# Second attention: output products in three passes behind the next pair's first scores, and all full key tiles split

## What is computed

```python
def rmsnorm(x, g): return x * rsqrt(mean(x*x) + 1e-5) * g
q = (layernorm(x) @ Wq).reshape(b, Sq, 16, 128)     # 256 queries a batch
k = (ctx @ Wk).reshape(b, Skv, 16, 128)             # 1601 keys a batch
v = (ctx @ Wv).reshape(b, Skv, 16, 128)
scores = einsum('bqhd,bkhd->bhqk', rmsnorm(q, gq), rmsnorm(k, gk)) * 128**-0.5
out = einsum('bhqk,bkhd->bqhd', softmax(scores), v)
x = x + tanh(g) * (out.reshape(b, Sq, 2048) @ Wo)
```

## Time and profile before

| | |
|---|---|
| median of 3 runs | 1923.51 us (1918.31 to 1924.34) |
| profiled execution: its own time, its span | 1915.69 us, 1914.0 us |
| TensorE / VectorE / ScalarE / GpSimd busy | 95% / 71% / 61% / 18% of the span |
| granted clock of TensorE, mean | 0.984 |

### The profile page before, as it was taken

How to read it: one execution, slowest core, us unless ns; L and a number is a source line. 1 busy time by engine, 2 the same in 40 slices (tenths; PEclk the granted TensorE clock), 3 DMA queues, 4 the chain that set the end, 5 groups by cost and what they waited for, 6 DMA issues and landing times.

```text
span 1914.0 us, 31506 instructions
## 1 busy us (share of the span) xinstructions
PE 1808.8 (95%) x9091; PEld 1327.3 (69%) x9091; DVE 1368.0 (71%) x2282; ACT 1165.7 (61%) x1946; POOL 340.1 (18%) x301
## 2 busy tenths in 40 slices
PE   5789898989999999999999999999999998999998
PEld 3344444558888677776777767777677776788887
DVE  8565656455665787887878878788688886666665
ACT  2576776843333677777877768777687774232232
POOL 3010101214443300001000010000100003444452
PEclk9899999989999999999999999999999998999999
DMA  3414232345443200001000010000000001455543
GB/s 97 108 30 96 54 72 51 75 160 132 112 112 79 69 1 0 0 0 35 1 0 0 0 35 1 0 0 0 1 1 0 0 0 47 102 115 115 113 111 77
DMA packets 108704, 95.80 MB, mean 50 GB/s; under 512 B 71796, under 2 KB 93176, under 8 KB 107992
## 3 DMA queue, kind: packets, MB, share of 16 engines
q1 hardware_dynamic: 108632, 94.88, 20.1%
HBM read 72.94 MB, written 1.44 MB: 39 GB/s over the span
## 4 chain that ended last, share of the span: by engine, by line
PE 80%; DVE 11%; ACT 2%; issue 2%; POOL 2%; SPq 1%; DMA 0%; ACTq 0%; DVEq 0%
PE ps L1213 28%; PE ps L451 17%; PE ps L462 8%; PE ps L1075 5%; PE ps L1287 4%; PE ps L1062 4%; PE ps L1308 3%; DVE s_rk L1847 3%; PE ps L1229 3%; PE ps L1000 2%; POOL s_p L786 2%; SPq L553 1%; PE ps L1303 1%; DVE s_rq L1843 1%; PE ps L1237 1%
## 5 line engine op out<-in xcount | busy, mean ns | idle before, releaser
L957 ACT ACTIVATE s_p<-ps,s_g,s_rk 128x256 f32<-128x256 f32 (+1 forms) x832 | 412.5, 560 | 120.3 <-PE ps L1213 91.1
L1213 PE MATMUL ps<-s_qq,s_ctxT 128*128 (+2 forms) x1248 | 385.4, 421 | 6.5 <-DVE s_qq L1836 5.0
L451 PE MATMUL ps<-s_xT,s_wgus 128*128 128x512 f32 x1440 | 349.9, 392 | 0.8 <-DVE s_hw L1740 0.8
L451 PEld LDWEIGHTS ps<-s_xT,s_wgus 128*128 128x128 f32 x1440 | 271.7, 189 | 60.1 <-DVE s_hw L1740 1.7
L1213 PEld LDWEIGHTS ps<-s_qq,s_ctxT 128*128 128x128 f32 (+1 forms) x1248 | 228.5, 184 | 93.0 <-issue 39.0
L1213 PE MATMUL ps<-s_ps,s_ctx 128*128 128x512 f32 x960 | 273.4, 394 | 0.1
L853 ACT ACTIVATE s_p<-ps,s_bsm 128x1024 f32<-128x1024 f32 x208 | 219.4, 1111 | 87.1 <-PE ps L1075 84.7
L1898 DVE TENSOR_TENSOR s_dsum<-s_dsum,s_p 128x512 f32<-128x512 f32 (+1 forms) x352 | 242.2, 688 | 26.8 <-ACT s_p L957 14.9
L1907 DVE TENSOR_TENSOR s_ps<-s_p,s_ps 128x512 fp32r<-128x512 f32 x320 | 220.0, 687 | 6.4 <-ACT s_ps L963 3.0
L1213 PEld LDWEIGHTS ps<-s_ps,s_ctx 128*128 128x128 f32 x960 | 180.0, 188 | 45.9 <-DVE s_ps L1907 1.8
L370 ACT CAST s_hs<-s_hw 128x512 fp32r<-128x512 f32 x120 | 74.5, 620 | 202.6 <-DVE s_hw L1740 202.6
(11 more groups left out here) (265 smaller groups left out, 2117.8 us busy)
## 6 DMA issues: line engine op xcount, KB each, us to landing
s_wB<-w1s SPq DMA_DIRECT2D x64, 256.0 KB, 3.9
s_kT<-s_kst SPq DMA_DIRECT2D x96, 128.0 KB, 2.3
s_kT<-s_kst SPq DMA_DIRECT2D x96, 80.0 KB, 2.1
s_wB<-w0s SPq DMA_DIRECT2D x15, 384.0 KB, 3.7
s_wB<-w0s SPq DMA_DIRECT2D x16, 256.0 KB, 3.9
s_wgu<-in_L_ffn_Wg_dram SPq DMA_DIRECT2D x64, 64.0 KB, 2.9
s_wgu<-in_L_ffn_Wu_dram SPq DMA_DIRECT2D x64, 64.0 KB, 2.6
s_wd<-in_L_ffn_Wd_dram SPq DMA_DIRECT2D x64, 64.0 KB, 2.6
```

The source lines that it names most:

```text
L451: ins = nc.tensor.matmul(ps[:, 4 + g, :], wgus[:, slot, w, g, k, :], xT[:, x_, k, n], start=c == 0, stop=c == len(ops) - 1)
L957: ins = nc.scalar.activation(p1[0:r, SLOT1[t], j, :], ps[0:r, BANK1[t], j * SQ:(j + 1) * SQ], ACT.Exp, bias=g1[0:r, 3:4], scale=rk_col(t, ...
L1213: ins = nc.tensor.matmul(out, lhs(x_), rhs(y_), start=first and n == 0, stop=last and n == 2)
```

## The change

1. **Tiles 3 and 7 are split too.** SPLIT1 is now tiles 0 to 11, only tile 12 stays plain. HI_DVE is tiles 1 and 6 (was 2, 6, 10), so ScalarE makes the high part of ten tiles (was seven). The ring ps1 has 4 slots (was 5).
2. **Output products in three passes.** oT1 becomes a high and a low part. ScalarE copies the high part from bank 4 (`take_sums`), VectorE subtracts for the low part (`low_sums`); it replaces VectorE's copy. M is kept in high and low parts, and the four plain matmuls become twelve float32r ones (line 1213's helper).
3. **They move.** TensorE's output products stand behind scores1(t = 3) of the next pair, ahead of scores1(4) and values1(0). ScalarE's copy stands behind the exponentials of tile 0 of the next pair and ahead of tile 0's high part. VectorE's subtraction stands first in the next pair. The first pair of a batch has none, and the last pair's stand behind the loop.
4. **M's parts ahead of the loop.** ScalarE copies eight high parts and four float32 copies (m1w); GpSimd subtracts for the first half (one instruction, 128 by 2048), VectorE for the second (four instructions of 512 columns, behind the layer norm). The layer norm's transposes use PSUM banks 4 to 7 instead of 0 to 3 and no longer wait for ScalarE's copies of M. One copy of ctx for each batch becomes smaller.

```diff
-SPLIT1 = (0, 1, 2, 4, 5, 6, 8, 9, 10, 11)
-HI_DVE = (2, 6, 10)
+SPLIT1 = tuple(range(KT - 1))
+HI_DVE = (1, 6)
-WHOLE1 = (3, 7, 12)
-RING1 = 5
+WHOLE1 = (12,)
+RING1 = 4
...
# GpSimd, ahead of the loop
+            pool.wait_ge(s.m1_read, 4)
+            n = slice(0, H1 * D // 2)
+            g_.tensor_tensor(m1[:, 1, n], m1w[:], m1[:, 0, n].bitcast(F32), ALU.subtract).then_inc(s.m1_rest, 1)
...
# ScalarE
+                def take_sums(hp):
+                    act.wait_ge(s.pv1, primed(at(KT * 8 * b, hp, KT, 0)))
+                    nc.scalar.copy(oT1[:, 0, :], ps[:, 4, :]).then_inc(s.o1_hi, 1)
...
                         ins.then_inc(s.probs1, 1)
+                        if t == 0 and not first:
+                            take_sums(hp)
                         if t in HI_ACT:
...
# TensorE
-            pe.wait_ge(s.m1_read, 8)
             pe_turn(pe, 2)
...
+                def outputs(hp):
+                    pe.wait_ge(s.o1_read, primed(hp + 8 * b))
+                    pe.wait_ge(s.y1_added, primed(hp + (8 * b - 1)))
+                    for j in range(4):
+                        ins = product(ps[:, 5 + j // 2, (j % 2) * D:(j % 2 + 1) * D], lambda part: oT1[:, part, j * P:(j + 1) * P],
+                                      lambda part: m1[:, part, bass.ds(hp * (2 * D) + (j // 2 - 2) * D, D)])
+                    ins.then_inc(s.y1_made, 1)
...
                         if t:
                             values1(hp, t - 1)
+                        elif not first:
+                            outputs(hp)
                     values1(hp, KT - 1)
...
-                    pe.wait_ge(s.o1_read, primed(hp + (8 * b + 1)))
-                    pe.wait_ge(s.y1_added, primed(hp + 8 * b))
-                    for j in range(4):
-                        ins = nc.tensor.matmul(ps[:, 5 + j // 2, (j % 2) * D:(j % 2 + 1) * D], oT1[:, j * P:(j + 1) * P],
-                                               m1[:].rearrange("p h n -> p (h n)")[:, bass.ds(hp * (2 * D) + (j // 2) * D, D)],
-                                               start=True, stop=True)
-                    ins.then_inc(s.y1_made, 1)
...
# VectorE
+            for j in range(4, 8):
+                n = slice(2 * D * j, 2 * D * (j + 1))
+                dve.wait_ge(s.m1_hi, j + 1)
+                v.tensor_tensor(m1[:, 1, n], ps[:, j % 4, :], m1[:, 0, n].bitcast(F32), ALU.subtract).then_inc(s.m1_low, 1)
...
+                def low_sums(hp):
+                    dve.wait_ge(s.o1_hi, at(8 * b, hp, 1, 0))
+                    v.tensor_tensor(oT1[:, 1, :], ps[:, 4, :], oT1[:, 0, :].bitcast(F32), ALU.subtract).then_inc(s.o1_read, 1)
...
                 def weights(hp, first):
+                    if not first:
+                        low_sums(hp)
                     for t in range(KT):
...
-                    dve.wait_ge(s.pv1, primed(at(k0, hp, KT, KT)))
-                    v.tensor_copy(oT1[:], ps[:, 4, :]).then_inc(s.o1_read, 1)
...
+                low_sums(H1 // 2)
                 finish(H1 // 2)
```

More of the change, by code:

```diff
@@ L270, in program @@
         p1 = sb("p1", [P, 5, 2, SQ], scope=se)
-        dsum = sb("dsum", [P, 2 * SQ], scope=se)
-        oT1 = sb("oT1", [P, 2 * SQ], scope=se)
-        m1 = sb("m1", [P, H1, D], scope=se)
+        m1 = sb("m1", [P, 2, H1 * D], F32R, scope=se)
         ctxT1 = sb("ctxT1", [P, 2, KV + 1], F32R, scope=se)
@@ L283, in program @@
         ps1 = sb("ps1", [P, RING1, 2, HALF], F32R, scope=se)
-        sb("ps1_rest", [P, H1 * P + KSQ * HALF - RING1 * 2 * HALF], scope=se)
+        dsum = sb("dsum", [P, 2 * SQ], scope=se)
+        oT1 = sb("oT1", [P, 2, 2 * SQ], F32R, scope=se)
         rd1 = sb("rd1", [P, 4], scope=se)
@@ L326, in program, with turn_bank @@
         of = out.rearrange("b s d -> (b s) d").rearrange("(t p) d -> p t d", p=P)
+        def turn_bank(k):
+            return 4 if k == 2 else 0
         def act_std(act, k, cols=slice(0, NT), half=0):
@@ L336, in act_take @@
                 act.wait_ge(s.ln_turned, 16 * k + 8 * half + 4 * (c + 1))
-                nc.scalar.copy(xnT[:, c, half * HALF:(half + 1) * HALF], ps[:, 2 * half + c, :]).then_inc(s.xnT_act, 1)
+                nc.scalar.copy(xnT[:, c, half * HALF:(half + 1) * HALF], ps[:, turn_bank(k) + 2 * half + c, :]).then_inc(s.xnT_act, 1)
         def act_turn(act, k):
@@ L410, in pe_turn_half @@
                 for t in range(4):
-                    nc.tensor.transpose(ps[:, 2 * half + c, t * P:(t + 1) * P], xn[:, 4 * half + t, c * P:(c + 1) * P],
+                    nc.tensor.transpose(ps[:, turn_bank(k) + 2 * half + c, t * P:(t + 1) * P], xn[:, 4 * half + t, c * P:(c + 1) * P],
                                         ident[:]).then_inc(s.ln_turned, 1)
@@ L947, in _, with exponentials @@
                 act.wait_ge(s.bound1_ready, 1)
-                with act.Fori(0, H1 // 2) as hp:
+                def take_sums(hp):
+                    act.wait_ge(s.pv1, primed(at(KT * 8 * b, hp, KT, 0)))
+                    nc.scalar.copy(oT1[:, 0, :], ps[:, 4, :]).then_inc(s.o1_hi, 1)
+                def exponentials(hp, first):
                     k = KT * 8 * b
@@ L963, in _ @@
                             nc.scalar.copy(ps1[:, SPLIT1.index(t) % RING1, 0, :], p1[:, SLOT1[t], :, :].rearrange("p a n -> p (a n)")).then_inc(s.p_hi, 1)
+                exponentials(0, True)
+                with act.Fori(1, H1 // 2) as hp:
+                    exponentials(hp, False)
+                take_sums(H1 // 2)
             if stages < 4:
@@ L1289, in values1, with pair @@
                     ins.then_inc(s.pv1, 1)
-                def pair(hp, following):
+                def outputs(hp):
[5 more added lines that the diff above has]
+                    ins.then_inc(s.y1_made, 1)
+                def pair(hp, first, following):
                     for t in range(KT):
@@ L1315, in _ @@
                 pe.wait_ge(s.qq_read, 4 * TB * (b + 1))
-                with pe.Fori(0, H1 // 2 - 1) as hp:
-                    pair(hp, True)
-                pair(H1 // 2 - 1, False)
+                pe.wait_ge(s.m1_rest, 1)
+                pair(0, True, True)
+                with pe.Fori(1, H1 // 2 - 1) as hp:
+                    pair(hp, False, True)
+                pair(H1 // 2 - 1, False, False)
+                outputs(H1 // 2)
             if stages < 4:
```

26 lines of the change are left out of this document (15 added, 11 removed).

## The result

| | before | after |
|---|---|---|
| median of 5 runs each | 1921.23 us (1918.31 to 1924.34) | 1943.69 us (1937.87 to 1945.76) |
| profiled execution: time, span | 1915.69 us, 1914.0 us | 1937.87 us, 1936.1 us |
| granted clock of TensorE, mean | 0.984 | 0.979 |

The ratio is 1.0118, 95% interval 1.0104 to 1.0133: the change makes the kernel 22.5 us slower by the medians, 22.2 us by the profiled executions. The forecast was 1936 us, 12.5 over the median of the three runs of the kernel before that were known then; two further runs have brought that median down by 2.3 us.

The account below looks back on a forecast made before the run. TensorE set the pace before; after, VectorE's in-order chain to values1(3) would stall it. 1915.7 + 10.1 + 1.2 + 1.6 - 0.1 = 1928.5; on the median 1923.5 + 12.8 = 1936 us, range 1915 to 1946.

Parts of the forecast that it names:

- the chain to values1(3): Ordinary pairs: values1(3) waits for low part 3 until u = 9.96 (u from values1(12)'s start); period 21.8 us, 0.36 longer.
- TensorE sets the pace: Rival, chance 0.12: in the pair loop low part 3 ends by u = 8.75 or sooner; period 20.9 to 21.0, 1912 us.
- twelve output passes in 1.5 us: TensorE's output products: twelve single passes over 256 columns take 1.5 us in all, saving 0.1 us.
- the pairs: Pair loop: the 7 pairs of a batch with a predecessor grow longer, 28 x 0.36 = +10.1 us.
- the first pairs: First pair of each batch: ScalarE's 1.63 per tile is slower than TensorE's 1.40; +0.3 us each, +1.2 us.
- Cost 0, hidden behind TensorE's query and key products: Ahead of the loop: GpSimd's subtraction delays its low part of ctx at no cost; 1 to 2 us once if uncovered.
- the batches' ends: Behind each batch's last pair: outputs and VectorE's additions come later, +0.4 us each, +1.6 us.
- the clock: Rival, chance 0.02: TensorE stands 5% of the loop and its granted clock falls, +25 us at worst.

Follow-up runs that it names:

- spread: Kernel after with finish cut into its four additions, behind low parts 2, 3, 5 and 8: 1917.20 us, ratio 0.9989 to the kernel before.
- ports: Kernel after with GpSimd's subtraction for M behind its first query scaling, and its low part of ctx waiting for VectorE's low part of ctxT: 1934.39 us, ratio 1.0085.
- late_rest: Kernel after with only GpSimd's subtraction for M moved behind its first query scaling: 1935.62 us, ratio 1.0085 to the kernel before.
- after_again: The kernel after, unchanged, run and profiled a second time: 1944.00 us, ratio 1.0129 to the kernel before.

## Why the prediction was right, and where not

**Right: the chain to values1(3).** Period 21.8 forecast, 21.67 measured; values1(3) at u = 9.96 forecast, 9.72 measured; the wait, its releaser and its place as said, the later tiles without a wait as said. spread shows it: the same work with finish in pieces loses the wait and 0.80 us a pair. The size was over by 0.13 in the period and 0.24 in u, handovers that I had put at 0.1 to 0.2 us each: sum 3 started at 8.36 for 8.5, TensorE 0.75 behind low 3's start for 0.86. The period is over by less than u because the way from values1(3) to values1(12) was too short in the forecast, 11.84 for a measured 11.99 (1299.30 - 1287.31): the product behind the stall takes 0.80 us, not 0.70. The rival "TensorE sets the pace" was one edit away: with low 3 at u = 7.30 the period is 20.87, where it named 20.9.

**Right: twelve output passes in 1.5 us.** 1281.70 - 1280.19 = 1.51. The estimate by the Trainium skill (TensorE: Matmul & The Clock Gate, § The mechanism), 2.6 us, under which a weight load would not overlap a matmul of the same rows, does not hold here: these passes start every 0.126 us. The same section also names a background weight buffer whose loads are pulled ahead; the prediction left that out, and the measured spacing agrees with it.

**Right in sum, wrong in parts: the pairs.** +10.1 forecast as 28 x 0.36; measured 24 x 0.225 and 4 x 0.98, together +9.3. That the sum came out is partly luck: a period shorter than forecast hides that I had not looked at the last pair of a batch, where VectorE's 1.20 a tile or ScalarE's 1.63 stand against TensorE's 0.70. Rows of both were at hand.

**Wrong: the first pairs.** +1.2 forecast, -0.5 measured in the profiled execution (19.96 for 20.1); in executions with a half-rate stretch there it is +1.0 each.

**Wrong: "Cost 0, hidden behind TensorE's query and key products" ahead of the loop.** This is the step that failed. It measured +5.2 us. The forecast put VectorE's new work at its own length, 2.4 us, and gave it a cover of 1.0 us. That part held: ports has this work ahead of the loop and a stretch of 6.54 us, as before. What the forecast did not ask is what GpSimd's new instruction does to VectorE beside it. late_rest and ports show the mechanism by its parts (11.73, 8.17, 6.54). The Trainium skill (SBUF — State Buffer, § SBUF: two separate sides) states it: a VectorE instruction with two SBUF inputs and a GpSimd instruction that reads SBUF exclude each other for the whole instruction. The trace agrees, for an instruction of one column too (3.67 us for 0.15); VectorE's own subtractions just ahead (line 1843), which read one operand from PSUM, are not held: the last three of the four take 1.88 us from start to end, though GpSimd's begins in their midst.

**Too small: the batches' ends.** +1.6 was forecast for four; measured +3.9 for three transitions and +0.3 behind the last. The outputs' start at u = 2.42 (2.55 forecast) was right, and so was the size of the forecast's own term: in ports each transition is 0.3 us longer than before, and VectorE's additions start at u = 4.2 for 3.9. (The forecast read today's additions at 3.74; counted from the start of values1(12) they stand at 3.91.) The rest of the 3.9 is VectorE held by GpSimd's low part of ctx again, some 2 us (ports has the stretch from query to key product back at 6.46 and 7.07 us), and 0.9 us in the one half-rate stretch at a batch's end.

**Not in the sum: the clock.** It was a rival with a chance of 0.02, as a fall inside the loop. There, in the ordinary pairs, it stayed at 1.00 in spite of TensorE's pause in every pair. It fell at the batches' edges, which costs 6.3 to 6.6 us in the usual executions beside the profiled one.

The forecast time was 8 us under the measured one and in the range, but of the 22.5 us by which the kernel became slower it foresaw 12.8. Of the 22.2 us between the profiled executions the largest part missed is the 5.3 us ahead of the loop, then 2.6 at the batches' ends; the pairs (0.8) and the first pairs (1.7) came out smaller than forecast and hide part of that. Another 3.8 us of the 22.2 lie ahead of and behind the second attention, mostly in stages that the change leaves alone, and the usual executions have 6.3 to 6.6 us more in half-rate stretches than the profiled one. So the sign and the largest term come from a chain that was read rightly; that the time lies in the range owes something to the range's width, and to a median of the kernel before that was 2.3 us high.

**Left open.** Why half-rate stretches stand at every edge in some executions of the kernel after and only in two places in another. spread's gain over the kernel after, 1.3% or some 25 us, is more than its loop (24 x 0.80 + 4 x 0.38 = 20.7). Against the usual executions the traces have the rest: from the first query product to the last values1(12) spread takes 945.61 us, after_again 970.07, and of these 24.5 us 2.2 lie in the first pairs and 1.3 at the ends of batches, where spread has fewer half-rate stretches. Whether an even TensorE keeps the clock up there was not shown: one profile of spread is all there is.

## What to carry over

When a product comes to need one more operand from another engine, list what stands ahead of that operand in that engine's instruction stream, and cut the long blocks there into pieces between tiles: moving the block whole only moves the stall, and here the pieces turned 1.0118 into 0.9989. Look at the edges of a loop apart from its body: the pair without a successor had another bound here. And where GpSimd gets an instruction, look at every VectorE instruction beside it that has two inputs in SBUF, however small, and at who waits for it.

## What the runs showed of the hardware

- A VectorE instruction on 128 by 1 elements took 3.67 us beside a GpSimd subtraction of 4.52 us, and 0.15 us without; one on 128 by 128 took 3.43 to 3.48 us beside one of 3.42 to 3.44, and 0.29 without.
- Twelve float32r passes of 256 columns with 128 rows, each with its own weights, took 1.51 us, 0.126 each.
- TensorE paused 0.5 to 0.8 us in every pair, and its granted clock in the loop stayed at 1.00 over 171 us; at the batches' edges the same pauses of 0.6 us stood ahead of stretches at 0.50 in after_again and not at batch 1's end in the profiled execution.
- In the kernel after, a first pair with a 3.4 us stretch at a granted clock of 0.50 took 21.0 to 21.1 us, one at 1.00 throughout 19.96.
